# Token loads three deep, expert weights on ScalarE's queue, and the routed experts' GpSimd and DVE programs written out

## The reference, cut to what matters

```python
def reference(x, cond_2048, Wq, Wo, router_w, gate_up_w, down_w, sh_gate_w, sh_up_w, sh_down_w):
    h = cond_attention(x, cond_2048, Wq, Wo)         # (16, 256, 512): 8 heads, masked, over the 512 columns
    t = h.reshape(4096, 512)                         # 4096 tokens
    shared = silu(t @ sh_gate_w) * (t @ sh_up_w) @ sh_down_w          # 512 -> 256 -> 512
    top_val, top_idx = top_k(t @ router_w, 2)        # 2 of 8 experts
    probs = zeros(4096, 8).at[arange, top_idx].set(sigmoid(top_val))
    xin = probs.T[:, :, None] * t[None]
    gate, up = split(einsum('etd,edf->etf', xin, gate_up_w), 2)       # per expert 512 -> 2 x 256
    expert_out = einsum('eti,eid->etd', silu(gate) * up, down_w)      # 256 -> 512
    return x + (shared + expert_out.sum(0)).reshape(16, 256, 512)
```

## Time and profile before

| | us |
|---|---|
| median of 3 runs | 1420.14 (1418.18 to 1421.29) |
| the profiled execution, its own time | 1418.52 |
| its span (first to last instruction) | 1416.8 |
| TensorE matmul busy | 1255.0 |
| DVE busy | 696.6 |
| ACT busy | 491.2 |
| POOL busy | 812.7 |

### The profile page before, as it was taken

One profiled execution on the slowest core, in us unless ns is written; L12 is line 12 of the kernel. 1 busy time (PEld: TensorE's weight loads), 2 busy tenths in 40 slices (PEclk: granted clock), 3 DMA queues, 4 the chain that ended last, 5 costly groups with the idle time before them and its releaser, 6 DMA issues. The chain is left out here.

```text
span 1416.8 us, 21922 instructions
## 1 busy us (share of the span) xinstructions
PE 1255.0 (89%) x5500; PEld 672.5 (47%) x5501; DVE 696.6 (49%) x1243; ACT 491.2 (35%) x922; POOL 812.7 (57%) x670
## 2 busy tenths in 40 slices
PE   5999999999999999997868877799999989888884
PEld 2444554555445545543867766344444434333331
DVE  4677776667676677761542323233333333333332
ACT  1556666566566565663311111111111111111110
POOL 1587877778877778787007710354555444444443
PEclk7899999999999999998888989799999999999997
DMA  6666566665567666551364565333444445455541
GB/s 174 169 180 168 167 165 176 183 189 169 160 170 190 174 167 168 144 146 55 121 230 137 182 221 183 104 112 121 132 142 144 146 150 164 156 156 169 162 167 52
DMA packets 116488, 221.86 MB, mean 157 GB/s; under 512 B 18974, under 2 KB 21790, under 8 KB 116448
## 3 DMA queue, kind: packets, MB, share of 16 engines
q1 hardware_dynamic: 91360, 164.55, 39.6%
q0 software_dynamic: 23936, 54.72, 12.8%
q10 hardware_dynamic: 1152, 2.10, 0.6%
HBM read 150.14 MB, written 90.00 MB: 169 GB/s over the span
## 5 line engine op out<-in xcount | busy, mean ns | idle before, releaser
L746 DVE TENSOR_REDUCE row_max<-bank 128x1 f32<-128x512 f32 x512 | 343.6, 684 | 175.1 <-PE bank L568 174.5
L681 ACT ACTIVATE probsT<-bank 128x512 f32<-128x512 f32 x512 | 300.3, 596 | 227.2 <-PE bank L580 225.1
L437 POOL TENSOR_TENSOR key_sum<-key_sum,probsT 128x1024 f32<-128x1024 f32 x128 | 299.7, 2374 | 0.4 <-ACT probsT L681 0.4
L568 PE MATMUL bank<-k_stack,q_stack 96*128 96x512 f32 x512 | 281.8, 554 | 11.4 <-DMA q_stack<-q_hi 6.5
L1533 PE MATMUL bank<-gate_up_sb,rows_T 128*128 x576 | 274.8, 600 | 1.7 <-ACT rows_T L1480 1.6
L433 POOL TENSOR_TENSOR key_sum<-probsT 128x1024 f32<-128x1024 f32 x64 | 151.3, 2375 | 128.2 <-ACT probsT L681 128.2
L580 PE MATMUL bank<-q_stack,k_stack 99*128 99x512 f32 x512 | 206.9, 405 | 1.7 <-ACT probsT L681 1.5
L568 PEld LDWEIGHTS bank<-k_stack,q_stack 96*128 96x128 f32 x512 | 98.2, 193 | 167.3 <-DVE row_max L746 126.6
L1487 ACT ACTIVATE gated<-bank 128x256 f32<-128x256 f32 x72 | 27.6, 384 | 406.5 <-PE bank L1533 406.5
L1552 PE MATMUL bank<-down_sb,act_hT 128*128 x288 | 144.9, 626 | 25.9 <-DVE act_hT L1439 25.5
L1533 PEld LDWEIGHTS bank<-gate_up_sb,rows_T 128*128 128x128 f32 x576 | 103.8, 192 | 110.7 <-issue 110.6
(11 more groups left out here) (143 smaller groups left out, 1508.6 us busy)
## 6 DMA issues: line engine op xcount, KB each, us to landing
expert_rows_dram<-zero_rows SPq DMA_DIRECT2D x16, 1152.0 KB, 7.2
expert_rows_dram<-rows_out SPq DMA_DIRECT2D x72, 256.0 KB, 2.0
k_stack<-hi_dram SPq DMA_DIRECT2D x60, 256.0 KB, 6.3
q_stack<-hi_dram SPq DMA_DIRECT2D x60, 256.0 KB, 7.1
x_row<-in_x SPq DMA_DIRECT2D x16, 512.0 KB, 3.5
rows_ext_dram<-hid SPq DMA_DIRECT2D x16, 512.0 KB, 5.7
tok<-rows_ext_dram SPq DMA_DIRECT2D x16, 512.0 KB, 6.6
x_in<-in_x SPq DMA_DIRECT2D x16, 512.0 KB, 5.4
```

Source lines behind the costliest of these rows:

```text
L437: nc.gpsimd.tensor_tensor(total, total, probs(k), ALU.add).then_inc(added, 1)
L568: nc.tensor.matmul(logit_bank[i % 2][:, :], q_stack[par][g][0:K_LOGIT, h, q * P:(q + 1) * P], k_stack[par][g][0:K_LOGIT, h, :], start=True ...
L681: nc.scalar.activation(probsT[:, j, :], key_bank[j % 2][:, :], ACT.Exp, scale=SCALE).then_inc(probs_ready, 1)
L746: nc.vector.tensor_reduce(row_max[g][:, i:i + 1], logit_bank[i % 2][:, :], AX.X, ALU.max)\
```

## The change

Of SP's and ScalarE's programs in block2: `tok` gets a third buffer, `load(b + 3)` is issued where `load(b + 2)` was, the weights of expert b - 1 are started by ScalarE after its work for b (b = 1 to 8), and the slot table is loaded ahead of the last store. Of block3: the GpSimd and DVE programs are written out for all 72 tiles, with n a number, so that indices and probabilities are read from `slot_info` itself; `row_info`, `link_info` and their copies are gone; `rows_in` has six buffers and gathers go three tiles ahead; gather_partners no longer waits for an earlier scatter. The other engines' loop takes two steps a round.

```diff
-            tok = fb("tok", [P, KD, T])
+            tok = [rb(f"tok{i}", [P, KD, T]) for i in range(3)]
...
                 def load(b):
-                    i = b % 2
-                    if b >= 2:
-                        sp.wait_ge(tok_turned, 2 * (b - 1))
+                    i = b % 3
+                    if b >= 3:
+                        sp.wait_ge(tok_turned, 2 * (b - 2))
...
+                load(2)
                 for b in range(B):
-                    if b + 2 < B:
-                        load(b + 2)
+                    if b + 3 < B:
+                        load(b + 3)
                     if b >= 1:
                         store(b - 1)
                         if b + 1 < B:
                             load_x(b + 1)
-                    if b % 2 == 1:
-                        load_expert(b // 2)
-                store(B - 1)
                 sp.wait_ge(scattered, 16 * 2 * TT)
                 sp.dma_start(slot_info[:, :, :], slot_table.rearrange("(p n) c -> p n c", p=P)).then_inc(info_loaded, 16)
+                store(B - 1)
...
                     silu(b)
                     upper_sh(b)
+                    if 1 <= b <= E:
+                        load_expert(b - 1)
...
-            DEPTH = 4
-            row_info = eb("row_info", [P, 2], I32, DEPTH)
-            link_info = eb("link_info", [P, 2], I32)
+            DEPTH = 6
+            AHEAD = 3
...
-                for n in range(DEPTH):
-                    step(n, n)
-                with eng.Fori(1, NT // DEPTH - 1) as n:
-                    for i in range(DEPTH):
-                        step(DEPTH * n + i, i)
+                for n in range(4):
+                    step(n, n % 2)
+                with eng.Fori(2, NT // 2 - 1) as n:
+                    for i in range(2):
+                        step(2 * n + i, i)
...
-                def gather(n, i):
-                    if not first(n, DEPTH):
+                def gather(n):
+                    if n >= DEPTH:
                         pool.wait_ge(out_ready, n - DEPTH + 1)
-                        passed()
-                    nc.gpsimd.tensor_copy(row_info[i][:, :], slot_info[:, bass.ds(n, 1), ROW:PROB + 1].rearrange("p o c -> p (o c)"))\
-                        .then_inc(row_info_ready, 1)
-                    pool.wait_ge(row_info_ready, n + 1)
-                    passed()
...
+                for n in range(AHEAD):
+                    gather(n)
                 for n in range(2):
                     nc.gpsimd.memset(partner_rows[n][:, :], 0.0).then_inc(partner_cleared, 1)
                 pool.wait_ge(partner_cleared, 2)
...
+                for n in range(NT + 2):
+                    if n + AHEAD < NT:
+                        gather(n + AHEAD)
+                    if 0 <= n - 2:
+                        scatter(n - 2)
+                    if 0 <= n - 1 < NT:
+                        gather_partners(n - 1)
```

More of the change, by code:

```diff
@@ L937, in build @@
             info_loaded = fsem("info_loaded")
-            tok_loaded = [fsem(f"tok_loaded{i}") for i in range(2)]
+            tok_loaded = [fsem(f"tok_loaded{i}") for i in range(3)]
             x_in_loaded = [fsem(f"x_in_loaded{i}") for i in range(2)]
@@ L1400, in scatter @@
                                                  bounds_check=TOKENS - 1, oob_is_err=False)\
[L1401 to L1409 removed]
+                        .then_inc(final_scattered[n % 2], 16)
@@ L1412, in _ @@
                 pool.wait_ge(partner_cleared, 2)
-                for n in range(2):
-                    gather(n, n)
-                tiles(pool, step)
+                for n in range(NT + 2):
[5 more added lines that the diff above has]
+                        gather_partners(n - 1)
                 for i in range(2):
@@ L1420, in _, with scale_rows @@
             def _(dve):
-                def scale_rows(n, i):
-                    dve.wait_ge(gathered[i], turns(n, i, DEPTH) + 16)
-                    if not first(n):
+                def scale_rows(n):
+                    dve.wait_ge(gathered[n % DEPTH], 16 * (n // DEPTH + 1))
+                    if n >= 2:
                         dve.wait_ge(in_turned, n - 1)
-                    nc.vector.tensor_scalar(rows_scaled[i % 2][:, :], rows_in[i][:, 0, :],
-                                            row_info[i][:, PROB:PROB + 1].bitcast(F32), None, ALU.mult).then_inc(scaled, 1)
@@ L1442, in add_rest @@
-                def add_rest(n, i):
+                    nc.vector.tensor_copy(act_hT[i][:, :, :],
+                                          hT_bank[i][:, 0:I].rearrange("p (k c) -> p k c", k=KI)).then_inc(h_copied, 1)
+                def add_rest(n):
                     dve.wait_ge(down_done, n + 1)
-                    if not first(n):
-                        dve.wait_ge(stored[i % 2], turns(n, i, 2))
-                    nc.vector.tensor_tensor(rows_out[i % 2][:, :], out_bank[i % 2][:, :], rows_in[i][:, 1, :], ALU.add)\
+                    if n >= 2:
+                        dve.wait_ge(stored[n % 2], 16 * (n // 2))
+                    nc.vector.tensor_tensor(rows_out[n % 2][:, :], out_bank[n % 2][:, :], rows_in[n % DEPTH][:, 1, :], ALU.add)\
@@ L1448, in add_rest @@
                         .then_inc(out_ready, 1)
-                def add_partner(n, i):
-                    dve.wait_ge(partner_gathered[i % 2], turns(n, i, 2) + 16)
-                    if not first(n):
-                        dve.wait_ge(final_scattered[i % 2], turns(n, i, 2))
-                    nc.vector.tensor_tensor(rows_final[i % 2][:, :], out_bank[i % 2][:, :], partner_rows[i % 2][:, :], ALU.add)\
-                        .then_inc(final_ready, 1)
-                def step(n, i):
-                    if exists(n - 2):
-                        add_rest(n - 2, (i - 2) % DEPTH)
-                    if exists(n - 1):
-                        copy_h(n - 1, (i - 1) % DEPTH)
-                    if exists(n - 2):
-                        add_partner(n - 2, (i - 2) % DEPTH)
-                    if exists(n):
-                        combine(n, i)
-                    if exists(n + 2):
-                        scale_rows(n + 2, (i + 2) % DEPTH)
@@ L1469, in _, with add_partner @@
-                dve.wait_ge(partner_cleared, 2)
-                for n in range(2):
-                    scale_rows(n, n)
-                tiles(dve, step)
+                def add_partner(n):
+                    dve.wait_ge(partner_gathered[n % 2], 16 * (n // 2 + 1))
+                    if n >= 2:
+                        dve.wait_ge(final_scattered[n % 2], 16 * (n // 2))
+                    nc.vector.tensor_tensor(rows_final[n % 2][:, :], out_bank[n % 2][:, :], partner_rows[n % 2][:, :], ALU.add)\
+                        .then_inc(final_ready, 1)
@@ new lines, in _ @@
+                for n in range(2):
+                    scale_rows(n)
+                dve.wait_ge(partner_cleared, 2)
+                for n in range(NT + 2):
+                    if 0 <= n - 2:
+                        add_rest(n - 2)
+                    if 0 <= n - 1 < NT:
+                        copy_h(n - 1)
+                    if 0 <= n - 2:
+                        add_partner(n - 2)
+                    if n < NT:
+                        combine(n)
+                    if n + 2 < NT:
+                        scale_rows(n + 2)
```

86 lines of the change are left out of this document (32 added, 54 removed).

## The result

The changed kernel takes 1296.4 us (median of 4 runs, 1294.7 to 1297.6) against 1419.2 us for the one before on the same chip. The ratio is 0.914, 95% interval 0.911 to 0.916. I had said 1322 us with a range of 1302 to 1364: faster was right, the gain was larger than my range allowed. The profiled execution has a span of 1292.6 us, 2.1 us around it, so the two profiled spans differ by 124.2 us, where I had 98.

What follows compares the result with a forecast made beforehand. Bound: TensorE's `tok` waits in the shared stage, then two GpSimd loops (row gather, later partner gather) in the experts. Gains 41 + 3 + 2 + 52 = 98 us from 1418.5 give 1321, stated as 1322 us; 8-in-10 range 1302 to 1364.

Steps and rivals of the forecast that it cites:

- The shared stage: Shared expert: six long periods become short, 45.4 us, less 4 us for periods that transfers stretch: 41 us gained.
- the 7.4 us: Shared stage, lower bound: at 300 GB/s a weight period is 10.5 us, six cost 7.4 us, leaving 38 us gain.
- rival A: Shared stage: transfers are the bound, 237 GB/s at most in a period; 24 us less gain, 1346 us; chance 0.13.
- the 3 + 2 forecast: Change of stage: 3 us from the last store's earlier landing, 2 us from issuing the first gather first.
- The tiles: Routed experts, 71 periods: 444 us against 497.5, 54 us less 2 for shorter loops' branches: 52 us gained.
- TensorE's 5.81 us: Routed experts: TensorE's floor for a tile; each tile takes the greater of this and the partner loop.
- The landing may grow: Partner gathers: landing lengthens as scatter and row gather come closer; 0.2 us taken, bounds 0 and 0.8.
- the 0.93 that I kept: Partner loop: 0.93 us between the semaphore and the scatter's start stay, being there without a copy too.
- the end of the row loop: Routed experts: gathers three tiles ahead into six buffers give the 4.3 us landing two periods, so this loop ceases to bind.
- B: Partner loop: 0.88 us belong to every indirect DMA waiting for semaphores; 37 us less gain, 1358 us; chance 0.12.
- D: Partner gather queues behind the row gather, 3.3 us added to each landing; slower, 1522 us; chance 0.04.
- C: Whole kernel: everything covered, no landing growth (9 us) and the full 45.4 us come (4 us): 1309 us; chance 0.15.

Runs made afterwards that it cites:

- tok3_only: Kernel before with three `tok` buffers and the slot table ahead of the last store, weights still on SP's queue, routed experts as before: 1374.3 us (0.968).
- the small store: Kernel before, with SP's store of each tile's sum moving 16 of 128 rows: late partner-gather landing 0.24 us shorter; total time not in the text.
- two_ahead: Changed kernel with gathers two tiles ahead into four buffers instead of three into six, still without index copies: total time the same as the changed kernel's.
- half_gather: Changed kernel whose row gather fetches half of each row, 256 KB instead of 512: no effect on landing that shows; total time not in the text.
- no_scatter: Changed kernel whose scatters move nothing from tile 9 on: late partner-gather landing about 0.12 us shorter; total time not in the text.
- partner_first: Changed kernel with GpSimd issuing the partner gather of tile n-1 ahead of the scatter of tile n-2: 1278.9 us (0.901).
- written_out: Changed kernel with index copies and waits back, gathers two ahead, four buffers: 18.7 us faster than the 1370.3 us with only the shared stage changed.

## Why the prediction was right in kind and wrong in size

*The shared stage* was right: 45.1 us went where I had 41. The 4 us that I took off for stretched periods did not come; the transfers had the room, 0.83 share over the stage. The bounds of this part counted six weight periods where the change has eight: the 7.4 us should have been 9.8, and rival A's 24 us 32; neither is in the forecast. Its reason held, too: `tok3_only` has all twelve short periods, with the weights still on SP's queue. Rival A, 237 GB/s as the most a period can hold, is out: the stage runs at 274 GB/s with no wait.

*End of the stage and start of the experts*: from the last copy of turned tokens to the first gather it was 25.1 us and is 19.5 (818.12 to 837.66): 5.6 us for the 3 + 2 forecast.

*The tiles* hold the miss. Between the first and the last `rows_final` 71.2 us went, and I had 52. By stretch, forecast and measured: first 22 tiles 127.8 and 127.8 (TensorE's 5.81 us, exact); middle 16 98.2 and 96.7; late 28 188.7 and 175.0; last 5 29.1 and 26.7; the branches of the shorter loops 2 and nothing, for the first 22 tiles are at the floor with them. My late period of 7.25 us before was a count in a window; the additions of tiles 38 and 66 are 206.1 us apart, 7.36 us a tile.

The step that failed is "The landing may grow ... I take 0.2 us, with bounds 0 and 0.8". It should have had a bound below nothing. I had argued that scatter and row gather come closer, which they do, and priced only that; the runs put 0.12 us on the one and nothing on the other. What I left out is the third neighbour, SP's store of `rows_out`: gathers three tiles ahead let it start ahead of the partner gather instead of right behind it, and it stops lengthening the landing. The row that I took for nearest, the step of the landing near 1177 us, I also read wrongly. I put it down to the row gather; it goes with the store, which moves there from 2.2 to 0.6 us behind the partner gather, and with the small store the step is 0.33 us instead of 0.57. On 28 tiles, 3.8 us taken and 3.40 measured are 11.2 us, half of it my 0.2 and half the fall by 0.19. Another 2.5 us are the scatter's start after its semaphore, 0.84 us instead of the 0.93 that I kept. The last 5 tiles went below TensorE's 5.81 us, which I had made a floor: their gathers move nothing, the loop is 5.0 us by its own steps, and TensorE had run ahead while the late tiles waited: its `down` of tile 66 ends 7.6 us ahead of that tile's `rows_final`, the one of tile 71 4.8 us. A floor holds for a stretch only if the engine has no lead to give back.

A second step was right by luck. I had put the end of the row loop down to the third tile of distance, and `two_ahead` shows that the missing copies alone all but end it (130.2 instead of 127.8 us for the first 22 tiles). The sum was not touched, since I priced one loop only after the other was gone.

Of the rivals, B is refuted by the rows: 0.30 us stand between scatter and partner gather. D too: the row gather behind costs nothing (`half_gather`). C, everything covered, 1309 us, was nearest, and the truth lies 13 us beyond it.

The last 2.1 us are at the end: behind the last `rows_final` the kernel before had 8.44 us, the changed one 6.31. In the old one the last scatter started 3.60 us after the end of its addition, now 0.83. I had no term for it. It is the place of a stall of GpSimd, told in the last section, that came just ahead of the last scatter and now comes within the last five tiles, whose 26.7 us are five times 5.0 and this stall.

## What to carry to other kernels

When work moves on one engine, write down for each transfer in the critical wait which other transfers cross it before and after, those of engines that do not move among them; the sign of the change of its landing is open until that is done. Where two loops run through one in-order engine, the chain of waits names the one that came last, not the one whose shortening pays: price both loops with the change in. And if a loop is addition, scatter, gather on one queue, ask whether the gather needs the scatter ahead of it; here the order of two lines was worth 17.6 us.

## What the runs showed of the hardware

An indirect DMA on GpSimd takes 1.0 us to issue. Its start comes 0.30 us after the one before it where its waits are satisfied; 0.79 to 0.88 us after a copy of its indices on the same engine; and 0.84 us after the end of another engine's instruction that it blocked on (0.95 as a mean of the late tiles where the program is a loop).

Twice in a kernel GpSimd stands idle between two indirect DMAs with nothing that it waits for, the first time for 1.8 to 3.3 us. In the changed kernel and in the one before:

```profile
1066.25 1.01 POOL L1374 DMA_INDIRECT out<-rows_final,slot_info  x1 [2.84 <-DVE rows_final L1432]
...
1069.23 1.03 POOL L1367 DMA_INDIRECT partner_rows<-expert_rows_dram,slot_info  x1 [1.97 <-issue]
```

```profile
1156.71 0.99 POOL L1370 DMA_INDIRECT rows_in<-rows_ext_dram,row_info  x1 [3.31 <-issue]
```

In each of the 14 kernels here the first falls right behind the 177th indirect DMA that GpSimd starts, the 64 scatters of the slot table counted. The second falls behind the 274th in the seven kernels that gather three tiles ahead, and behind the 279th in the seven that gather two ahead, at whatever time and in loops as in written-out programs. `no_scatter` and `partner_first` have a third, 2.5 us, behind the 92nd. What these stalls are was not tried.

The Trainium skill (Runtime: NRT & Kernel Launch, "Instruction fetch mechanics") says that straight code is fetched ahead in blocks and that a taken branch can stall. No run here tests that alone. The shorter loops of the other engines cost nothing that the first 22 tiles, exactly at 5.81 us, would show; and the 0.5 us a tile that `written_out` gains in them can be register instructions as well as branches.
